# Local attention in another slot order: odd heads' row sums on VectorE, their normalising on ScalarE, q, k and masks side by side, v a tile later

## The reference, cut to what matters

```
# x here is ln(x): 16 sequences of 512 tokens; the window is 64
h = shift_token(x); q, k, v = split(h @ wqkv)        # 8 heads of 64
q, k = l2norm(q) * qs, l2norm(k) * ks
q, k = rotary_xpos(q, k)                             # q also carries the factor 8
sim  = q @ k^T, each row over its own window of 64 and the one before
attn = softmax(sim)                                  # masked outside the band
x = x + (attn @ v) @ wo
h = layernorm(shift_token(x)); a, g = split(h @ w1 + b1)
x = x + (a * gelu(g)) @ w2 + b2
```

## Time and profile before

| what | value |
|---|---|
| median of 3 runs | 2631.54 us (2631.46 to 2634.67) |
| the profiled execution's own time | 2637.19 us |
| its span | 2635.6 us |
| granted TensorE clock, mean | 0.986 |
| local attention, layer 0, first to last transpose of `hs` | 1310.1 to 1815.9 us |
| local attention, layer 1, first to last transpose of `hs` | 1978.3 to 2470.1 us |

### The profile page before, as it was taken

The page is one execution under the profiler, slowest core; times in us unless marked ns, Lnnn a source line. Parts: engine busy times, 40 slices in busy tenths (PEclk is TensorE's granted clock), DMA queues, the critical chain, the costliest instruction groups (busy, mean ns, idle before and its releaser), DMA issues.

```text
span 2635.6 us, 71253 instructions
## 1 busy us (share of the span) xinstructions
PE 2543.2 (96%) x24208; PEld 1991.5 (76%) x24208; DVE 2005.9 (76%) x5640; ACT 2155.1 (82%) x6334; POOL 1665.7 (63%) x1974
## 2 busy tenths in 40 slices
PE   6999999999999999999899899998998999999899
PEld 4777777777777777777678788887786888888777
DVE  4667666667666666666589899998568999999865
ACT  5888888888888888888589899999447999999844
POOL 3544444444444444444489889998237999999743
PEclk9999999999999999999999999999899999999999
DMA  2000000000000000000112311111201111111121
GB/s 74 6 13 9 10 5 9 6 9 9 10 5 9 5 10 10 9 6 5 38 37 46 101 38 38 42 40 30 70 17 41 44 43 38 43 38 41 27 69 53
DMA packets 131878, 76.13 MB, mean 29 GB/s; under 512 B 83700, under 2 KB 114240, under 8 KB 131520
## 3 DMA queue, kind: packets, MB, share of 16 engines
q1 hardware_dynamic: 122896, 67.31, 10.7%
q10 hardware_dynamic: 8624, 4.27, 0.6%
HBM read 16.99 MB, written 8.41 MB: 10 GB/s over the span
## 4 chain that ended last, share of the span: by engine, by line
PE 45%; issue 2%; POOL 1%; DVE 1%; ACT 1%; SPq 1%; DMA 0%; DVEq 0%; POOLq 0%; ACTq 0%
PE bank L1275 5%; PE bank L1241 5%; PE bank L1254 5%; PE bank L1206 4%; PE bank L1297 4%; PE bank L1220 4%; PE bank L1207 3%; PE bank L1208 3%; PE bank L1449 3%; PE bank L1229 2%; PE bank L1440 2%; PE bank L1441 2%; PE bank L1442 2%; PE bank L866 1%; POOL f_qkr L981 1%
## 5 line engine op out<-in xcount | busy, mean ns | idle before, releaser
L319 POOL TENSOR_SCALAR L<-L,rinv 128x128 f32<-128x128 f32 (+3 forms) x1024 | 525.5, 536 | 599.4 <-DVE rinv L511 599.4
L391 ACT ACTIVATE L<-L,nmax 128x384 f32<-128x384 f32 (+3 forms) x1024 | 572.9, 563 | 139.7 <-DVE nmax L497 139.7
L497 DVE CUSTOM_DVE_ANT_0 L<-bank,f_rows 128x256 f32<-128x256 f32 (+3 forms) x1024 | 470.3, 479 | 171.9 <-PE bank L613 170.1
L1037 ACT ACTIVATE f_L<-bank,f_nmax,f_rn 128x128 f32<-128x128 f32 x1024 | 460.0, 483 | 4.3 <-DVE f_nmax L1162 4.2
L999 POOL TENSOR_TENSOR f_rn<-f_ssq,f_mhalf 128x16 f32<-128x16 f32 x128 | 419.1, 3274 | 20.4 <-DVE f_ssq L1146 7.2
L981 POOL TENSOR_TENSOR f_qkr<-f_rows 128x256 f32<-128x256 f32 x512 | 417.0, 845 | 22.1 <-DVE f_rows L1113 22.1
L634 PE MATMUL bank<-ident,L 128*128 128x128 f32 x2560 | 370.3, 276 | 2.3 <-DVE PT L216 2.0
L634 PEld LDWEIGHTS bank<-ident,L 128*128 128x128 f32 x2560 | 297.9, 141 | 82.7 <-issue 44.9
L1113 DVE TENSOR_TENSOR f_rows<-bank,f_rows 128x512 f32<-128x512 f32 x512 | 348.0, 680 | 8.3 <-ACT f_sq L1027 8.3
L655 PE MATMUL bank<-PT,v 128*64 128x512 f32 (+3 forms) x2048 | 303.9, 439 | 0.6 <-DVE yacc L532 0.4
L655 PEld LDWEIGHTS bank<-PT,v 128*64 128x64 f32 x2048 | 126.8, 136 | 165.9 <-issue 164.6
(11 more groups left out here) (157 smaller groups left out, 6461.0 us busy)
## 6 DMA issues: line engine op xcount, KB each, us to landing
f_vm<-f_v SPq DMA_DIRECT2D x224, 128.0 KB, 2.4
xb<-in_L_attn_x SPq DMA_DIRECT2D x16, 256.0 KB, 2.9
out<-yacc SPq DMA_DIRECT2D x32, 128.0 KB, 1.8
f_hs<-xf SPq DMA_DIRECT2D x128, 32.0 KB, 1.9
out<-f_acc ACTq DMA_DIRECT2D x16, 256.0 KB, 2.3
f_hs<-xf SPq DMA_DIRECT2D x128, 28.0 KB, 1.8
L<-bias_rows SPq DMA_DIRECT2D x4, 512.0 KB, 7.5
f_hs<-xf SPq DMA_DIRECT2D x128, 3.8 KB, 1.9
```

Of the source, the lines that this page charges most:

```text
L319: nc.gpsimd.tensor_scalar(t, t, rinv[:, h % RING, a, i:i + 1], 1.0, ALU.mult, ALU.mult).then_inc(s_N, 1)
L391: nc.scalar.activation(t, t, ACT.Exp, bias=nmax[:, ep % RING, a, i:i + 1], scale=-1.0, accum_out=rsum[:, ep % RING, a, i:i + 1]).then_inc( ...
L497: nc.vector.tensor_tensor_reduce(out=L[:, p % RING, a, LOFF[i]:LOFF[i] + (i + 1) * P], in0=ps_s[a][i], in1=bias_tab[:, 2 * p + a, T - (i + ...
L1037: nc.scalar.activation(L[:, ot % 2, a, k, :], ps_s[a][:, k * P:k * P + P], ACT.Exp, bias=nmax[:, ot % 2, a, k:k + 1], scale=rn[:, ot % 2, ...
```

## The change

No instruction of the computation is left out. What differs:

- The exponents of the odd heads no longer accumulate their row sums. DVE sums them with one tensor_reduce over 128x512 (`osum`), waits for it, and inverts.
- The odd heads' probabilities are normalised on ACT: four 128x128 copies with `rinv` as scale. The 128x512 multiplication on DVE (L1151) is gone.
- Every engine's list is in another order. PE projects q and k of `now` behind the values, then writes the masks one slot early; v is projected for `two` instead of `one`. ACT copies v out for `three`, the probabilities for `four`, OT for `five`. POOL does `rn` first, for `two`, then the four rotations of `one`. DVE does three table products ahead of the maxima, and `kr` right behind `nmax`.
- SP waits for v of three tiles back instead of two before it issues the copies to `vm`, and so before the next slot's load of `hs`.

```diff
...
         sp.wait_ge(sem["hT_done"], at(b, TT, t - TT + 1))
         load_shifted(sp, hs, xf, b, t, sem[f"hs{t}"])
...
+    three = tile_back(b, t, 3)
+    if three is not None:
+        vb, vt = three
         sp.wait_ge(sem["v_out"], at(vb, TT, vt + 1))
...
         if vt < TT - 1:
...
         sp.dma_start(w["acc"][:], d["out"].rearrange("b (t p) d -> p (b t) d", p=P)).then_inc(w["s_acc"], 16)
-tile_slots(sp, slot, lag=2)
+tile_slots(sp, slot, lag=3)
 for b in range(2):
...
 sp.wait_ge(s, 16 * 12)
...
             nc.gpsimd.tensor_tensor(halves(qkr[:, tt % 2, k], s), halves(ab[:, tt % 2, k, 0], s),
...
                                         sem[("q_rotated", "k_rotated")[k]], 1)
-    rotate(1, two)
+    if two is not None:
+        tb, tt = two
+        r = tt % 2
+        pool.wait_ge(sem["ssq"], at(tb, TT, tt + 1))
+        for n in ("exp_even", "exp_odd"):
+            pool.wait_ge(sem[n], at(tb, FC * TT, FC * (tt - 1)))
+        pool.wait_ge(sem["kr"], at(tb, TT, tt - 1))
+        nc.gpsimd.tensor_tensor(rn[:, r, :], ssq[:, r, :], w["mhalf"][:], ALU.pow).then_inc(sem["rn"], 1)
     rotate(0, one)
+    rotate(1, one)
     if three is not None:
...
         pool.wait_ge(sem["rinv_even"], at(tb, TT, tt + 1))
-        a = L[:, tt % 2, 0]
-        nc.gpsimd.tensor_tensor(a, a, rinv[:, tt % 2, 0].unsqueeze(2).to_broadcast([P, FC, P]),
+        p = L[:, tt % 2, 0]
+        nc.gpsimd.tensor_tensor(p, p, rinv[:, tt % 2, 0].unsqueeze(2).to_broadcast([P, FC, P]),
                                 ALU.mult).then_inc(sem["probs_even"], 1)
...
     if l == 0 and 8 <= b < 12:
...
             pool.sem_clear(n)
...
     act.wait_ge(m["hn"], TT * B)
 def slot(b, t):
-    now, one, two, three, four = (tile_back(b, t, k) for k in range(5))
+    now, one, two, three, four, five = (tile_back(b, t, k) for k in range(6))
     def square(k):
...
+        if one is None:
+            return
+        ib, it = one
+        act.wait_ge(sem[("q_done", "k_done")[k]], at(ib, TT, it + 1))
+        act.wait_ge(sem["ssq"], at(ib, TT, it - 1))
+        nc.scalar.activation(sq[:, it % 2, k, :], (ps_q, ps_k)[k][:], ACT.Square).then_inc(
             sem[("q_squared", "k_squared")[k]], 1)
...
+    def exps(a, ks):
+        if three is None:
+            return
+        ob, ot = three
         act.wait_ge(sem["nmax"], at(ob, TT, ot + 1))
         act.wait_ge(sem["PT_done"], at(ob, 2 * TT, 2 * (ot - 1)))
-        for k in range(FC):
+        for k in ks:
+            how = {"accum_out": rsum[:, ot % 2, 0, k:k + 1]} if a == 0 else {}
             nc.scalar.activation(L[:, ot % 2, a, k, :], ps_s[a][:, k * P:k * P + P], ACT.Exp,
                                  bias=nmax[:, ot % 2, a, k:k + 1], scale=rn[:, ot % 2, 2 * k + a:2 * k + a + 1],
-                                 accum_out=rsum[:, ot % 2, a, k:k + 1]).then_inc(sem[("exp_even", "exp_odd")[a]], 1)
+                                 **how).then_inc(sem[("exp_even", "exp_odd")[a]], 1)
+    def normalise_odd():
+        if four is None:
+            return
+        ob, ot = four
+        act.wait_ge(sem["rinv_odd"], at(ob, TT, ot + 1))
+        for k in range(FC):
+            p = L[:, ot % 2, 1, k, :]
+            nc.scalar.activation(p, p, ACT.Copy, scale=rinv[:, ot % 2, 1, k:k + 1]).then_inc(sem["probs_odd"], 1)
     def rotated_out(k):
         if two is None:
...
             sem[("qT_out", "kT_out")[k]], 1)
     def probs_out(a):
-        if three is None:
-            return
-        ob, ot = three
+        if four is None:
+            return
+        ob, ot = four
         act.wait_ge(sem["PT_done"], at(ob, 2 * TT, 2 * ot + a + 1))
...
         nc.scalar.activation(PT[:, a].rearrange("p k q -> p (k q)"), ps_t[a][:], ACT.Copy).then_inc(sem[f"PT_out{a}"], 1)
+    square(0)
+    square(1)
+    if three is not None:
+        vb, vt = three
+        act.wait_ge(sem["v_done"], at(vb, TT, vt + 1))
+        for n in ("pv_even", "pv_odd"):
+            act.wait_ge(sem[n], at(vb, TT, vt - 2))
+        nc.scalar.activation(v[:, vt, :], ps_v[:], ACT.Copy).then_inc(sem["v_out"], 1)
+    if five is not None:
+        xb, xt = five
+        act.wait_ge(sem["pv_even"], at(xb, TT, xt + 1))
+        act.wait_ge(sem["pv_odd"], at(xb, TT, xt + 1))
+        act.wait_ge(sem["wo_done"], at(xb, TT, xt))
+        nc.scalar.activation(OT, ps_o[:].rearrange("p (c q) -> p c q", c=FC), ACT.Copy).then_inc(sem["OT_out"], 1)
+    normalise_odd()
+    probs_out(0)
+    probs_out(1)
     if now is not None:
...
         nc.scalar.activation(hT_hi[:, t % 2, :], ps_q[:, 0:P], ACT.Copy).then_inc(sem["hT_hi"], 1)
-    exps(1, three)
+    exps(1, (0, 1))
+    exps(0, (0, 1, 2, 3))
+    rotated_out(1)
+    exps(1, (2, 3))
     rotated_out(0)
...
     if (b, t) == (B + 1, 0):
...
         batch_affine(nc, act, c, w, l, 0)
...
         nc.vector.tensor_reduce(rmax[:, a, :], ps_s[a][:].rearrange("p (k j) -> p k j", k=FC), AX.X,
                                 ALU.max).then_inc(sem["rmax"], 1)
...
     table_product(0, 0)
+    table_product(0, 1)
+    table_product(1, 0)
     maxima(0)
...
         dve.wait_ge(sem["rn"], at(ob, TT, ot + 1))
-        for a in ("exp_even", "exp_odd"):
-            dve.wait_ge(sem[a], at(ob, FC * TT, FC * (ot - 1)))
+        for n in ("exp_even", "exp_odd"):
+            dve.wait_ge(sem[n], at(ob, FC * TT, FC * (ot - 1)))
         nc.vector.scalar_tensor_tensor(out=nmax[:, ot % 2], in0=rmax[:], scalar=-1.0,
...
                                        op0=ALU.mult, op1=ALU.mult).then_inc(sem["nmax"], 1)
...
     if two is not None:
...
         dve.wait_ge(sem["rn"], at(ib, TT, it + 1))
...
         kr = qkr[:, it % 2, 1].rearrange("p (h e) -> p h e", h=FH)
...
                                 ALU.mult).then_inc(sem["kr"], 1)
+    if five is not None:
+        xb, xt = five
+        dve.wait_ge(sem["wo_done"], at(xb, TT, xt + 1))
+        p = xf[:, bass.ds(xb * TT + xt, 1), :].squeeze(1)
+        nc.vector.tensor_tensor(p, ps_o[:, 0:D], p, ALU.add).then_inc(sem["x_out"], 1)
     table_product(1, 1)
+    if now is not None:
+        dve.wait_ge(sem["hT_hi"], at(b, TT, t + 1))
+        nc.vector.tensor_tensor(hT_lo[:, t % 2, :], ps_q[:, 0:P], hT_hi[:, t % 2, :].bitcast(F32),
+                                ALU.subtract).then_inc(sem["hT_lo"], 1)
+    sums(0, one)
     inverse(0, three)
+    sums(1, one)
+    if one is not None:
+        ib, it = one
+        dve.wait_ge(sem["ssum"], at(ib, 2 * TT, 2 * it + 2))
+        dve.wait_ge(sem["rn"], at(ib, TT, it - 1))
+        nc.vector.tensor_scalar(ssq[:, it % 2, :], w["ssum"][:], 1.0e-24, None, ALU.max).then_inc(sem["ssq"], 1)
+    if three is not None:
+        tb, tt = three
+        dve.wait_ge(sem["exp_odd"], at(tb, FC * TT, FC * tt + FC))
+        nc.vector.tensor_reduce(rsum[:, tt % 2, 1, :], L[:, tt % 2, 1], AX.X, ALU.add).then_inc(sem["osum"], 1)
+        dve.wait_ge(sem["osum"], at(tb, TT, tt + 1))
+    inverse(1, three)
     if (b, t) == (B, 0):
...
     if (b, t) == (B, 2):
...
             last = nc.tensor.transpose(ps_t[k][:, n * P:n * P + P], qkr[:, ot % 2, k, n * P:n * P + P], ident[:])
         last.then_inc(sem[("qT_done", "kT_done")[k]], 1)
...
+    def masks():
+        if two is None:
+            return
+        ob, ot = two
         for a in range(2):
...
                              skip_group_check=True)
+    def scores():
+        if three is None:
+            return
+        ob, ot = three
         pe.wait_ge(sem["qT_out"], at(ob, TT, ot + 1))
...
         if (l, ob, ot) == (0, 0, 0):
...
         if four is None:
...
         tb, tt = four
-        pe.wait_ge(sem[("probs_even", "probs_odd")[a]], at(tb, TT, tt + 1))
+        if a == 0:
+            pe.wait_ge(sem["probs_even"], at(tb, TT, tt + 1))
+        else:
+            pe.wait_ge(sem["probs_odd"], at(tb, FC * TT, FC * tt + FC))
         if three is not None:
...
         for k in range(FC):
...
                     if k == FC - 1 and half == 1:
                         last.then_inc(sem[("pv_even", "pv_odd")[a]], 1)
...
+    probs_T(0)
     scores()
-    probs_T(0)
+    if two is not None:
+        ib, it = two
+        pe.wait_ge(sem["v_out"], at(ib, TT, it))
+        project(2, ps_v, two).then_inc(sem["v_done"], 1)
     probs_T(1)
+    if now is not None:
+        pe.wait_ge(sem[f"hs{t}"], at(b, shifted_count(t), shifted_count(t)))
+        if one is not None:
+            ib, it = one
+            pe.wait_ge(sem["q_squared"], at(ib, TT, it + 1))
+            pe.wait_ge(sem["q_products"], at(ib, TT, it + 1))
+        nc.tensor.transpose(ps_q[:, 0:P], hs[:, t, :], ident[:]).then_inc(sem["hT_done"], 1)
     if five is not None:
         xb, xt = five
...
         for k in range(FC):
...
         last.then_inc(sem["wo_done"], 1)
-    if one is not None:
-        pe.wait_ge(sem["v_out"], at(ib, TT, it))
-        project(2, ps_v, one).then_inc(sem["v_done"], 1)
     rotated_T(0, two)
+    rotated_T(1, two)
+    values()
     if now is not None:
-
```

(8 more changed lines are left out.)

79 lines of the change are left out of this document (1 added, 78 removed).

## The result

| | kernel before | changed kernel |
|---|---|---|
| median | 2632.22 us (2631.46 to 2634.67) | 2732.77 us (2729.59 to 2733.18) |
| ratio | | 1.0378, 95% interval 1.0360 to 1.0396 |
| the profiled execution's own time | 2637.19 | 2729.59 (span 2728.0) |
| mean granted TensorE clock | 0.986 | 0.991 |
| local attention, first to last transpose of `hs`, layer 0 / 1 | 505.8 / 491.8 | 552.9 / 541.0 |

The change makes the kernel 3.8% slower, 100 us. The forecast was 2717 us, +3.2%, and the measured time lies inside the forecast's range.

A forecast was written before the change was run, and what follows sets the result against it. ScalarE was to bound: its list of 8.11 us plus a wait of 0.46 gives a period of 8.57, 0.71 over 7.86. 120 slots x 0.71 = 85 us, forecasting 2717 us (+3.2%), range 2652 to 2765.

The forecast's parts named there:

- ScalarE's list: ScalarE's instructions in one slot of local attention, summed from starts: 8.11 us after the change, 0.26 over the old period.
- the wait between neighbours: ScalarE's idle before the second copy out (L1070), waiting for TensorE's odd transposes, which need the last normalising copy: 0.46 us.
- The copies L1050: Four new ScalarE normalising copies, 128 columns with a per-partition scale: 0.16 base plus 0.09 operand, 0.25 each, 1.00 in all.
- The odd exponents: Four ScalarE exponents losing their accumulator read but keeping two operands: 0.34 instead of 0.435 each, saving 0.38 in all.
- Rival 4: On ScalarE, an exponent without the read still costs 0.435: period 8.95, 2763 us, chance 0.09.
- Rival 1: ScalarE without the wait, odd transposes coming in time: period 8.11, 2662 us, chance 0.08.
- The other engines all fit: VectorE, GpSimd, TensorE and SP all have to fit into a period of 8.57, and do, at no cost.
- The order's loop: Named after the experiments: squares, three VectorE table products, maxima, `nmax`, ScalarE's eight exponents and two copies, then the next square.
- Masks a slot early and v a tile later ... nothing: TensorE's reordered masks and v only give it work while others are late: no effect on time.
- Rival 2: Operand price hidden; VectorE's clamp `ssq`, waiting for GpSimd's even product, closes a loop: 8.08, 2658 us, chance 0.10.
- B's ring: The loop of Rival 2: VectorE's clamp `ssq` held by GpSimd's even product, closed through the rotations, 8.08.
- Rival 3: As Rival 2 but the clamp takes 0.17, so TensorE's list alone counts: period 7.79, 2623 us, chance 0.07.

The follow-up runs named there:

- e3: Changed kernel with the four normalising copies of the odd heads at scale 1 instead of the reciprocal, odd heads not normalised: 2686.20 us.
- e4: Changed kernel with ScalarE's four normalising copies moved ahead of the copy OT, so OT stands between them and the copies out: 2686.41 us.
- e6: Changed kernel with e4's move, and k's first table product on VectorE moved from ahead of the maxima to behind x_out: 2690.73 us.
- e9: e6 with TensorE's scores ahead of the even transposes and VectorE's clamp ssq behind the odd heads' sums and reciprocal: 2688.94 us.
- e7: Changed kernel with e3's edit and e4's move together, odd heads not normalised: 2686.65 us.

## Why the prediction was right, and where not

**What bounds.** ScalarE's list and the wait between neighbours: right. e3 took away part of the list and e4 the wait. The period followed to within 0.01 in e3 (8.37 forecast, 8.38), where a second bound lay at the same place, and until the next loop in e4.

**The copies L1050.** The mis-sized term. I took 0.16 for the base from `hT_hi`, which reads PSUM, and the new copies read SBUF: 0.200. With the operand's 0.093 (right) that is 0.293 for 0.25, inside the bounds of 0.16 and 0.34. 4 x 0.043 = 0.17, and 8.57 + 0.17 = 8.74 is the measured period to the last digit. Local attention had no small ScalarE instruction from SBUF before, but causal attention had, in the same trace: exponents of 128x128, from SBUF to SBUF, with one per-partition operand.

```profile
901.55 0.40 ACT L391 ACTIVATE L<-L,nmax 128x128 f32<-128x128 f32 x1
901.84 0.19 ACT L391 ACTIVATION_READ_ACCUMULATOR L<-L,nmax 128x1 f32 x1
```

The accumulator read starts 0.29 behind the exponent, 0.292 as the median of all 256. That is the new copy's price, and it stood outside the stretch that was read.

The rule of the Trainium skill, "ScalarE: Activation LUTs", section "What ACT_TABLE_LOAD costs", had said 0.29 for this copy, and the trace agrees. Its base is too high for the plain 512 columns, which come from PSUM, and right for 128 from SBUF. Its 0.39 for the odd exponent, also from PSUM, is not borne out: 0.342.

**The odd exponents.** 0.34, right; so was the reasoning from the start of the accumulator read and not from its duration. Rival 4 falls.

**The wait.** 0.46, right. e4 shows it to be what the forecast said, a ring of two neighbours that one copy put between them opens. The size owes something to luck. From the start of the last normalising copy to the second copy out pass 1.24, where 1.19 was forecast: the copy is done after 0.50 and not 0.39, and the rest takes 0.74 and not 0.80 (the transposes 0.66 in it, so that the 0.11 added for the first weight load, an estimate with no row behind it, was about twice too much). Without the wait it would be 0.77 and not 0.73, because of the 0.043, so the difference came out right. Rival 1 falls.

**"The other engines all fit", and the order for nothing.** Wrong as a reason, right for the sum only because something larger lay above. The order's loop is 8.34 in the change and 8.71 with the old division. "Masks a slot early and v a tile later ... nothing" missed that the order sets rings: squares to table products to maxima to exponents, and exponents to masks to scores to the copies out. I had summed lists and followed the one ring on which I expected the wait. The opening's sentence that a list's length is the period of a tile has the same fault: it holds only where no ring is longer.

**Rival 2** had the right coupling with 8.08, but the wrong ring as the nearest. Its own ring has `nmax` in it, at 0.17 where 0.46 was measured; 8.08 + 0.29 = 8.37, which is where e6 stands, though e6 also has ScalarE's 0.11 and e9, with a short clamp, stays there too. Whether B's ring by itself bounds anywhere stays open. Rival 3 was given too much with 0.07: e7, without the operand's price and without the wait, stays at 8.37, so that no road to "faster" was open.

**The sum.** 120 x 0.71 = 85 against +92.4 in the profiled executions. The period adds 120 x 0.17 = 21. 116 full intervals for 120, and ramps 5.7 us shorter together, take 9 back (116 x 0.886 - 5.7 = 97.1; measured 96.3), the rest of the program 4. The other 9 us between 2717 and 2732.77 are no fault of the mechanism: I carried over that the profiled execution lay 5.7 above the median, and after the change it lies 3.2 below. The profiled execution of the kernel before had a mean clock of 0.986; that kernel's other runs at 0.986 took 2634.6 to 2635.1 us, and those at 0.989 about 2631 to 2633.

**What was to be seen.** ScalarE "near 94%" busy came out at 96.9, since busy time counts overlapping durations; TensorE under 100, `rn` at 2.92, the idle of 0.26 before the second L1070, VectorE's idle before the even reciprocal, and SP's unchanged stall are all there.

**The parts don't add.** The division alone costs 1.14 per slot, the order alone 0.86, both together 0.89. A period is the longest of several rings, not their sum. The division shortens the order's loop by 0.37 (the odd exponents), and the order shortens the division's ring by 0.25 (8.99 to 8.74, as the scores and v stand between the even and the odd transposes): each part takes back some of what the other costs.

## What to carry to other kernels

In a hand-written software pipeline sum every ring that returns to its own engine within one slot, not only each engine's list: write down for each engine the one instruction that waits last, follow its releaser until the ring closes, and do this again for the new order. Price a new instruction from a row with the same kind of source (SBUF or PSUM) and the same operands, and from starts, not durations. Where producer and consumer on one engine have only a short trip to another engine between them, put an independent instruction of that length in between; and before moving a step that looks stretched, look at what its output starts.
